# Perceiver, RWKV and gated-expert block on one core: fourteen constant products, a later column fetch, and a new order of work on all engines

## The reference, cut to what matters

```python
x = x + xattn(layernorm(x), ctx_1024, ...)   # ctx: (2, 2048, 512)
x = x + rwkv(layernorm(x), ...)
x = x + experts(layernorm(x), ...)

def xattn(x, context):                # weights all 512 x 512
    z = causal_self_attn(x, Wq1, Wk1, Wv1);  x = layer_norm(x + z, ln1_g, ln1_b)
    z = cross_attn(x, context, Wq2, Wk2, Wv2); x = layer_norm(x + z, ln2_g, ln2_b)
    z = relu(x @ fc1_w + fc1_b) @ fc2_w + fc2_b
    return layer_norm(x + z, ln3_g, ln3_b)

def rwkv(inp):      # two time steps (one per sequence), 8 heads of 64
    xr, xw, xk, xv, xa, xg = (x + (xprev - x) * m for m in (mu_r, mu_w, mu_k, mu_v, mu_a, mu_g))
    r, k, v = xr @ Wr, xk @ Wk, xv @ Wv
    w = exp(-exp(-softplus(-(w0 + xw @ Ww)) - 0.5)); a = sigmoid(a0 + xa @ Wa); g = sigmoid(xg @ Wg)
    ...                               # state update, per-head norm, bonus term
    h = layernorm(inp + (y * g) @ Wo, norm_w, norm_b)
    return layernorm(silu(h @ Wf + bf), lnf_w, lnf_b)

def experts(x):     # 8 heads of 64, 5 experts, the best 2 chosen per row and head
    v = mix of the chosen x @ Wv[e];  attn = softmax(q k / 8) v
    return sum over chosen e of attn @ Wo[e]
```

## Time and profile before

| | before |
|---|---|
| median of 3 runs | 237.63 us |
| profiled execution, its own time | 238.05 us |
| its span on the chip | 236.3 us |
| TensorE busy | 225.8 us (96% of the span) |
| VectorE busy | 163.6 us (69%) |
| ScalarE busy | 92.6 us (39%) |
| GpSimd busy | 79.0 us (33%) |
| share of the last chain on TensorE | 89% |
| data moved | 43.99 MB |

### The profile page before, as it was taken

The page is one execution under the profiler, slowest core; times in us unless marked ns, Lnnn a source line. Parts: engine busy times, 40 slices in busy tenths (PEclk is TensorE's granted clock), DMA queues, the critical chain, the costliest instruction groups (busy, mean ns, idle before and its releaser), DMA issues.

```text
span 236.3 us, 3055 instructions
## 1 busy us (share of the span) xinstructions
PE 225.8 (96%) x1136; PEld 160.5 (68%) x1136; DVE 163.6 (69%) x310; ACT 92.6 (39%) x190; POOL 79.0 (33%) x78
## 2 busy tenths in 40 slices
PE   6799999999999999999999999999999699999994
PEld 5795968888978778588564444444444279799951
DVE  2243665598788996791275545889987889998961
ACT  2131417174439857912213444393712221251300
POOL 5032003144805453773060114746223116360000
PEclk9999999999999999999999999999999999999999
DMA  6999599805489199404999199300000000000011
GB/s 190 420 426 397 193 426 433 363 3 180 177 315 395 28 420 423 198 0 172 426 424 395 42 316 427 158 0 0 0 0 1 0 3 0 0 3 1 3 44 44
DMA packets 6351, 43.99 MB, mean 186 GB/s; under 512 B 832, under 2 KB 832, under 8 KB 1472
## 3 DMA queue, kind: packets, MB, share of 16 engines
q1 hardware_dynamic: 6336, 43.80, 46.6%
HBM read 43.27 MB, written 0.52 MB: 185 GB/s over the span
## 4 chain that ended last, share of the span: by engine, by line
PE 89%; DVE 4%; DMA 3%; ACT 2%; issue 1%; SPq 0%; POOL 0%; DVEq 0%
PE psum L401 67%; PE psum L442 17%; PE psum L405 3%; DMA ring<-blocks 3%; ACT slots L1485 2%; PE psum L416 1%; PE psum L547 1%; DVE small L858 1%; DVE slots L870 1%; DVE psum L1004 0%; DVE slots L876 0%; DVE slots L882 0%; DVE psum L1114 0%; DVE slots L1226 0%; DVE small L860 0%
## 5 line engine op out<-in xcount | busy, mean ns | idle before, releaser
L401 PE MATMUL psum<-ring,slots 128*128 128x512 f32 (+3 forms) x228 | 90.8, 546 | 1.4 <-ACT slots L1485 1.3
L401 PEld LDWEIGHTS psum<-ring,slots 128*128 128x128 f32 (+1 forms) x228 | 39.6, 190 | 42.1 <-issue 36.0
L1485 ACT ACTIVATE slots<-psum 128x256 f32<-128x256 f32 (+4 forms) x58 | 24.5, 447 | 84.2 <-PE psum L401 37.7
L401 PE MATMUL psum<-ring_r,slots_r 128*128 128x512 f32 x192 | 46.2, 396 | 0.0
L1791 POOL TENSOR_TENSOR ring_r<-ring,ring_r 128x640 fp32r<-128x640 f32 x16 | 32.7, 2059 | 35.0 <-ACT ring_r L1485 35.0
L401 PEld LDWEIGHTS psum<-ring_r,slots_r 128*128 128x128 f32 x192 | 35.5, 188 | 9.1 <-ACT slots_r L1485 1.0
L442 PE MATMUL psum<-slots,ring 128*128 128x128 f32 x320 | 40.4, 289 | 1.2 <-DMA ring<-blocks 0.9
L442 PEld LDWEIGHTS psum<-slots,ring 128*128 128x128 f32 x320 | 39.3, 204 | 1.9 <-ACT slots L1485 1.8
L1485 ACT ACTIVATE ring_r<-ring 128x2048 fp32r<-128x2048 f32 x16 | 30.5, 1913 | 14.9 <-DMA ring<-blocks 9.2
L888 DVE TENSOR_TENSOR ring_r<-ring,ring_r 128x1408 fp32r<-128x1408 f32 x16 | 28.7, 1801 | 4.0 <-ACT ring_r L1485 4.0
L1786 POOL TENSOR_TENSOR small<-small,mhalf 128x1 f32<-128x1 f32 x16 | 8.8, 553 | 64.5 <-DVE small L862 64.5
(11 more groups left out here) (170 smaller groups left out, 231.8 us busy)
## 6 DMA issues: line engine op xcount, KB each, us to landing
ring<-blocks SPq DMA_DIRECT2D x36, 1024.0 KB, 10.5
bc<-vecs SPq DMA_DIRECT2D x1, 3072.0 KB, 11.6
bc<-vecs SPq DMA_DIRECT2D x1, 1280.0 KB, 6.7
slots<-xin SPq DMA_DIRECT2D x2, 256.0 KB, 4.6
bc<-vecs SPq DMA_DIRECT2D x1, 512.0 KB, 17.0
y<-slots SPq DMA_DIRECT2D x2, 256.0 KB, 2.0
colv<-cols SPq DMA_DIRECT2D x1, 14.0 KB, 2.4
```

Source lines behind the costliest of these rows:

```text
L401: return t.matmul(o_, l, r, start=first, stop=last)
L1485: return a.activation(o, x, func, **kw)
```

## The change

The reference, the data and all single steps stay as they are. There are four kinds of edit:

1. PE makes 14 constant products at the front instead of 8.
2. SP fetches `colv` after `ct01` instead of ahead of `k1`. DVE's reader of it, `rest`, moves from behind the first norm to behind the first affine step.
3. The lists of all five engines are written in another order, with the same calls (the same number of each).
4. The names in the flags follow the lists. They change no instruction.

The lists' edits, cut to what the prediction speaks of:

```diff
@@ SP @@
             eng.dma_start(X[0], xin[0, :, :]).then_inc(s_x[0], 16)
-            eng.dma_start(colv[:, :], cols).then_inc(s_cols, 16)
             fetch("k1")
             eng.dma_start(X[1], xin[1, :, :]).then_inc(s_x[1], 16)
             fetch("q1")
             fetch("ct01")
+            eng.dma_start(colv[:, :], cols).then_inc(s_cols, 16)
             fetch("v1")
-            fetch("ct02")
+            fetch("q2")
             fetch("ct00")
             eng.dma_start(bc[:, 0:2, :], spread(0, 2)).then_inc(s_bc0, 16)
+            fetch("ct02")
+            eng.dma_start(bc[:, 2:FIRST_BC, :], spread(2, FIRST_BC)).then_inc(s_bc1, 16)
             fetch("k2")
-            fetch("q2")
+            fetch("ct03")
+            fetch("ct10")
             fetch("ct11")
-            eng.dma_start(bc[:, 2:FIRST_BC, :], spread(2, FIRST_BC)).then_inc(s_bc1, 16)
...
+            fetch("fq")
+            s.wait_ge(*used("c13"))
+            fetch("rw")
+            fetch("rr")
+            fetch("rk")
+            fetch("rg")
+            fetch("fk")
+            fetch("rv")
+            fetch("fo")
             s.wait_ge(*normed[0].at("n4"))
             s.wait_ge(*normed[1].at("n4"))
             eng.dma_start(bc[:, 0:len(BCAST) - FIRST_BC, :], spread(FIRST_BC, len(BCAST))).then_inc(s_bc2, 16)
-            fetch("rr")
-            fetch("fk")
-            fetch("fo")
-            fetch("rg")
+            fetch("ro")
+            s.wait_ge(*out_v[1].at("fin"))
+            eng.dma_start(out[1, :, :], X[1]).then_inc(s_y[1], 16)
             s.wait_ge(*out_v[0].at("fin"))
             eng.dma_start(out[0, :, :], X[0]).then_inc(s_y[0], 16)
-            s.wait_ge(*out_v[1].at("fin"))
-            eng.dma_start(out[1, :, :], X[1]).then_inc(s_y[1], 16)
@@ PE @@
             s.wait_ge(*const.at("ones"))
-            for _ in range(8):
+            for _ in range(14):
                 mm(psum[:, 7, 0:128], ones[:, :], ones[:, :], True, True)
...
+            q1(1)
+            em(0)
             k1(1)
-            em(0)
-            q1(1)
             pv1(0)
+            v1(1)
             e1(1)
-            v1(1)
...
             f1(1)
-            f2(1)
-            turned_rows(0, "n4", N4[0], 0)
             s.wait_ge(*p_low[0].at("3"))
             s.wait_ge(s_bc1, 16)
             bias("a0", 1)
             s.wait_ge(*p_low[1].at("3"))
             s.wait_ge(*evict[1].at("relu"))
             bias("a0", 6)
+            turned_rows(0, "n4", N4[0], 0)
+            f2(1)
             step(0, "a", 0, 1, bias_of="a0")
...
             fo(0, 0)
             fo(0, 1)
-            fo(0, 2)
             sum_u(1, 0)
             sum_u(1, 1)
+            sum_u(1, 2)
             fo(1, 0)
-            sum_u(1, 2)
             fo(1, 1)
             fo(1, 2)
+            fo(0, 2)
@@ DVE @@
             norm(0, "x", Y[0], X[0])
-            s.wait_ge(s_cols, 16)
-            v.tensor_scalar(rest, colv[:, 0:24], -1.0, 1.0, ALU.mult, ALU.add).then_inc(*rest_v.inc("rest"))
             start(1)
+            norm(1, "x", Y[1], X[1])
             k1_out(0)
-            norm(1, "x", Y[1], X[1])
...
+            affine(0, "x1", Z[0], TMP[0], "ln1_b")
+            s.wait_ge(s_cols, 16)
+            v.tensor_scalar(rest, colv[:, 0:24], -1.0, 1.0, ALU.mult, ALU.add).then_inc(*rest_v.inc("rest"))
+            s.wait_ge(s_bc1, 16)
+            v.tensor_scalar(kh, kh, 0.5, None, ALU.mult).then_inc(*own_v.inc())
             energies(1)
...
-            final(0)
             final(1)
+            final(0)
@@ ACT @@
+            split("c12")
+            copy_turned(0, "pc", T16, 3)
+            share_out()
             p_out(1, 3)
-            copy_turned(0, "pc", T16, 3)
-            p_out(1, 2)
-            split("c11")
-            split("c12")
             split("c13")
             row_high("a0", (s_bc1, 16))
+            p_out(1, 2)
             gathered(1)
```

More of the change, by code:

```diff
@@ L1312, in _ @@
             start4(0)
+            row_low("a0")
             norm(0, "n4", N4[0], X[0])
@@ L1406, in _ @@
             v.tensor_scalar(ssq[1], ssq[1], 0.0, 0.00064, ALU.max, ALU.add).then_inc(*rk_v[1].inc("e"))
-            bonus(1)
+            s.wait_ge(*evict[0].at("g"))
+            s.wait_ge(*rk_v[0].at("yb"))
+            v.scalar_tensor_tensor(out=ys[0], in0=g_p[0], scalar=1.0, in1=ys[0], op0=ALU.add,
+                                   op1=ALU.mult).then_inc(*rk_v[0].inc("yg"))
+            s.wait_ge(*own_v.now())
+            v.tensor_tensor(heads(ys[1]), heads(vc[0]), over(keep["al"], 64), ALU.mult).then_inc(*own_v.inc())
             s.wait_ge(*own_v.now())
@@ L1474, in _ @@
             gate_out(1, 2, 1)
+            final(1)
             final(0)
-            final(1)
         @block_.scalar
@@ L1849, in _ @@
             mul(x2b[0], Z[0], vec("fc2_b"), x2b_g[0], "x2b", ALU.add)
+            g.memset(tie[:, :, :], -TINY).then_inc(*own_g.inc())
+            for base in (0, -8):
+                s.wait_ge(*own_g.now())
+                i = g.affine_select(out=sel, in_=sel, compare_op=ALU.not_equal, fill=-1.0, base=base,
+                                    pattern=[[-1, 8]], channel_multiplier=1)
+                i.then_inc(*(const.inc("sel") if base else own_g.inc()))
             deviation(1, "x2")
```

348 lines of the change are left out of this document (163 added, 185 removed), and 4 rows, old and new, of the table prod.

## The result

The changed kernel takes **234.88 us** (median of 4 runs, 234.56 to 235.15) against 237.61 for the kernel before (4 runs in the same series, 237.38 to 238.65): ratio 0.987, 95% interval 0.9835 to 0.9905. The forecast was 236.0. The direction was right, the gain larger than forecast: 2.73 us between the medians, where 1.6 was forecast (237.63 to 236.0). The profiled execution took 235.15 with a span of 233.4, against 238.05 and 236.3 before: 2.90 us less, where the sum had 2.06.

The account below looks back on a forecast made before the run. TensorE was taken as the bound, busy 225.8 of 236.3 us, with a slow clock at the front. Minus 3.16 + 0.1 + 0.15 + 0.5 + 0.1 - 0.25 + 0.2 + 0.3 = minus 2.06 from 238.05 gave 236.0; range 234.7 to 238.0.

Parts of the forecast that it names:

- The front: Start to `q1`'s end of half 0: with the clock up and `colv` later, 15.25 instead of 18.41, 3.16 us won.
- Point 1: L1253 on DVE, waiting for late vectors, stands ahead of `energies(1)`, which feeds TensorE's count product: cost 0.1 us.
- Point 2: Penalty of half 1, before TensorE's L547: a split and a piece of P now stand ahead: cost 0.15 us.
- Point 3: Second layer norm of half 0: x2 late on DVE, cost 0.5 us, plus 0.1 for the last gather's third part.
- Point 4: `n4` of half 0: `f2(1)` behind the bias products hides ACT's mixing: minus 0.25 us.
- Point 5: `yg` of half 1: `sum_bonus(0)` waits for POOL amid DVE's work, with no slack: cost 0.2 us.
- Point 6: The end: `final(0)` starts 0.2 late and its store goes right behind that of `final(1)`: cost 0.3 us.
- The leaks: Places after the front where the gain can be lost, points 1 to 6 together: 1.1 us.
- the waits eat the gain: Rival: waits at points 1 to 6 cost 2.9 us, giving 237.8, no change; chance 0.20.
- the clock that stays low: Rival: clock not up in time between the products and `k1`, which ends 0.6 late: 239.75 us, slower; chance 0.08.
- the waits fit into the slack: Rival: of the losses only the end remains and `n4` gains, giving 234.8 us; chance 0.14.
- the 1.8 us piece: TensorE's wait behind L866, before the transposes of `n5` of half 0, forecast to stay unchanged.

Follow-up runs that it names:

- e1: Changed kernel with 8 constant products at the front instead of 14: 235.66 us, ratio 0.988 to the kernel before.
- e3: Kernel before with `colv` fetched after `ct01` and `rest` behind the first affine step, 8 products: 235.94 us, ratio 0.994.
- e13: Changed kernel with eight products and early `colv`, so the new lists alone: 238.47 us against 238.56 for the kernel before, ratio 1.010.
- e14: Kernel before with two constant products ahead of the transposes of `n5` of half 0: 237.39 us against 238.56, ratio 1.001.
- e11: Changed kernel with `penalty(1)` ahead of VectorE's `p_split(0,1)` again instead of behind it: 239.23 us.
- e12: Changed kernel with TensorE's old order around `n4` of half 0, ScalarE still mixing `k` ahead of `a`: 237.83 us.
- e15: Changed kernel with TensorE's old order around `n4` of half 0 and ScalarE's old order, `a` before `k`: 234.96 us.
- e7: Kernel before with 14 products, late `colv`, seven products ahead of `n5` of half 0, and new lists and stores from there on: 233.90 us, ratio 0.986.
- e5: Changed kernel with six more constant products ahead of the transposes of `n5` of half 0: 235.05 us.
- e4: Kernel before with both front edits, 14 products and the late `colv`, in the old lists: 235.91 us, ratio 0.988.
- e8: The changed kernel itself timed once more, nothing altered: 234.92 us.
- e2: Kernel before with 14 constant products and nothing else: 235.63 us, ratio 0.997.
- e9: Changed kernel with `colv` fetched ahead of `k1` again: 236.65 us, ratio 0.993.
- e10: Kernel before with 14 products, late `colv` and two constant products ahead of the transposes of `n5` of half 0: 234.41 us.

## Why the prediction was right and wrong

*The front: minus 3.16 forecast, minus 3.52 in the trace.* The mechanism stood in the main: the clock is up when `k1` begins, and `colv` no longer holds up `k1`'s block. But I had taken the number of products for what lifts the clock, and e1 and e3 had it up with eight. Both lack the wait for `k1`'s block; e13 and e14, with eight products and both idle pieces, ran the front slowly like the kernel before. `k1` started at 7.48, not 7.9, since the transposes followed the products at once and nothing waited for a block; the 64 records took 7.41, as I had from half 1 (7.34).

*Point 1, `energies(1)`*: 0.1 forecast, 0.11 measured from `q1`'s end to the first `shut_out`.

*Point 2, the penalty of half 1*: 0.15 forecast, 0.57 measured, of which 0.17 came back by `v2(0)`. I took L978's 0.48 us from the earlier trace rows; it took 1.43 with GpSimd's pieces (L1791) running beside it. The trace before had shown this already for half 0, where L978 took 1.45 us (at 61.04) beside a GpSimd addition. e11 shows that the obvious repair is worse.

*Point 3, x2 of half 0*: 0.5 and 0.1 forecast, 0.11 measured. This was the largest loss in my sum, and it was mis-sized, though x2 was nearly as late as I had said: its transposes started at 105.53, only 2.56 us earlier than before, 0.36 less than the lead at the gather ahead of them (96.59 against 99.51, 2.92). But 0.35 came back at once, as TensorE no longer waits for ACT at the transposes behind them (106.03 against 108.94, a lead of 2.91). I had named this wait and taken off only 0.1 for it. GpSimd's addition to X[1] came first, as I had feared, but was all but over when L876 began. L876 took 0.90 us instead of 0.74 and ended 0.55 behind it. By the rule of the Trainium skill ("SBUF — State Buffer", "Who interferes with whom") the later of the two waits for the other's end. The trace agrees to 0.2 us, since L876 alone takes 0.74 and ended 0.55 behind. So the price is what is left of the other's instruction, here 0.16 us, and not the 1.1 that I had put down by that rule.

*Point 4, `n4` of half 0*: minus 0.25 forecast, plus 0.22 measured. The sign was wrong. The bias products started at 122.56, that is 125.46 in the old times and not 125.2 (`row_low("a0")` was ready nearly when I said, but 0.15 us pass from VectorE's end to TensorE's start), and behind them the transposes waited 0.19 for the norm (L866), which I had left out. And the gain of 0.25 had rested on hiding these waits. e12 and e15 show that both engines' new orders together are worth nothing against both old ones, and that TensorE's old order with ScalarE's new one costs 3 us.

*Point 5, `yg` of half 1*: 0.2 forecast; 0.20 was gained before half 0's and 0.41 lost before half 1's. The sum is right by luck, since I had not seen the gain.

*Point 6, the end*: plus 0.3 forecast, minus 0.43 measured. This is the step that failed, with 0.73 of the 0.85 us by which the profiled execution missed 236.0: I looked only at the last product and the stores. From 219.30 to 233.12 TensorE needed 13.82 us before, from 216.84 to 230.23 now 13.39. No wait shows in either; the same products run in ten groups before and in six now, because `av`, `sum_u` and `fo` change less often. Behind the last matmul both take 3.2 us, so the two stores close together cost nothing of the 0.3. e7 confirms the 0.4; that the number of changes is its cause was not tried apart.

The leaks were 0.62 instead of 1.10 and the front 0.36 more: together the 0.85 us by which the profiled execution beats 236.0. Apart from the end, the errors nearly cancel: point 3 was 0.49 too dear and the front 0.36 too small a gain, while points 2 and 4 were 0.25 and 0.48 too cheap. That is luck. The median of the changed kernel lies another 0.27 us below its profiled execution.

*The rivals.* That the waits eat the gain was wrong, and its slower cousin, the clock that stays low, was not seen in the three profiled ones of the 18 executions of the changed kernel with and without filling (one of the others, e5's 235.97 us at a granted clock of 0.991, may have lost some time so). The time is that of "the waits fit into the slack" (234.8), but not by its mechanism: five waits did come, and the tail paid them back.

*What I did not see at all.* The sum holds for two executions. The medians are made by chance: whether the clock is up when `k1` begins, and whether it falls later, mostly behind an idle piece of 1.5 us or more. I said that the 1.8 us piece would stay and priced it at its own length. It shrank to 1.5, and that seems to be worth more than 0.3 us: in the old lists the drop behind it cost 1.7 more in seven executions of ten (e4), in the changed kernel in none of ten. By the medians, the lists alone gave 0.1 us (e13), the two front edits alone 2.4 (e4), and all together 2.9 (e8 against its series); by the ratios e4 is 1.2% and e8 1.0% faster than the kernel before, and e13 1.0% slower, which its interval doesn't tell from no change. The kernel before can do it as well: its fastest execution took 234.23 us, at a granted clock of 1.00. The rule cited from the Trainium skill ("TensorE: Matmul & The Clock Gate", "Part 1: The HAM clock gate"), that the number of slow matmuls differs from run to run, was the right warning, and the runs agree: the 64 records of the front took between 7.38 us (e2) and 10.19 us (the kernel before). I used it for the range and not for the median.

Open: why e9's slower executions are slow, why two executions with idle pieces of the same length differ, why the clock fell at 219 us in e13, and what the kernel before loses in the executions at a granted clock of 0.985, since its only profile is of one at 0.999.

## What to carry to other kernels

A TensorE wait of over a microsecond can cost its length and then as much again in half-speed matmuls behind it, so look at the granted clock just behind each wait, over several executions, before pricing it. Look also at the clock far from any wait. Two constant products in such a wait made the time both lower and steady in one version here (e10 against e4); in the changed kernel six gained nothing, and in the kernel before the gain of two isn't shown. When single moves of a hand-written order are undone, undo the other engines' half too: a move on one engine is often only the partner of a move on another.

## What the hardware showed that was not expected

- The granted clock is no matter of the front alone. It fell in the middle of the program behind idle pieces of 1.47, 1.66, 1.78 and 2.09 us (e15, e11, e4, e12) and stood at about half for 3 to 7 us. Each time TensorE had run at the high level for tens of microseconds before. It also fell at 219 us in e13, with TensorE busy without a gap for the 29 us before.
- It can come up and be lost again within the first 8 us (e13: rows at the high level at 6.27, clock at 0.62 from 7 us, 0.52 from 9).
- At the very front the column of the granted clock reads 1.00 while the pace is 7 records a microsecond, the 1.2 GHz level (the kernel before, up to 14 us); only behind a first rise does it follow the pace (e13: 0.52 with 12 records in the two microseconds from 9).
- VectorE's L978 on 4 partitions took 0.47 to 0.48 us alone and 1.15 to 1.85 us beside a running GpSimd (both in the kernel before: 0.48 at 81.02 us, 1.45 at 61.04).
